# Delta layer: the filter table loaded in four parts, five places to build the filter matrices in, and the key rows of half 0 turned after the filters

## The reference

```
x: [8, 512, 256]; 4 heads of 64; chunks of 32 tokens, 16 to a sequence
q, k, v = silu(conv4(norm(x) @ Wq)), ...              # q, k also scaled to length 1 per head
A  = strictly_lower(-(beta*k) @ k.T); T = inv(1 - A)  # one 32x32 system per sequence, chunk, head
u  = T @ v; w = T @ (beta*k); then a scan over the 16 chunks with the state S
s, m, l = depthwise causal filters of 3, 15, 63 taps over v
out = norm(gate-weighted sum of s, m, l, v and the scan's result) @ Wo
```

## Time and profile before

| | us |
|---|---|
| median of 3 runs | 4577.64 |
| profiled execution | 4567.55 |
| its span | 4565.8 |
| PE busy in the span | 3829.3 (84%) |
| DVE busy | 2545.7 (56%) |
| POOL busy | 2020.5 (44%) |
| ACT busy | 1897.9 (42%) |
| end of the last filter of half 0, of half 1 | 290.0, 509.6 |

### The profile page before, as it was taken

The page is one execution under the profiler, slowest core; times in us unless marked ns, Lnnn a source line. Parts: engine busy times, 40 slices in busy tenths (PEclk is TensorE's granted clock), DMA queues, the critical chain, the costliest instruction groups (busy, mean ns, idle before and its releaser), DMA issues. The chain is left out here.

```text
span 4565.8 us, 70606 instructions
## 1 busy us (share of the span) xinstructions
PE 3829.3 (84%) x26088; PEld 2661.1 (58%) x26088; DVE 2545.7 (56%) x4540; ACT 1897.9 (42%) x3440; POOL 2020.5 (44%) x2061
## 2 busy tenths in 40 slices
PE   5677796799999519958999799788888888999995
PEld 2555774466767319943544455466666666656663
DVE  5566563455454582247777432498888887412223
ACT  3224132333333202225666412488888886112222
POOL 3531463323232216632332211298999998332223
PEclk8788897899999859978999999899999999999997
DMA  4774642200000529954544210111111111822224
GB/s 113 234 226 137 199 120 74 84 5 19 10 19 6 173 70 295 297 152 135 151 138 137 65 63 28 51 50 41 49 47 52 52 47 52 278 92 45 46 46 131
DMA packets 333687, 459.66 MB, mean 101 GB/s; under 512 B 70838, under 2 KB 245366, under 8 KB 329222
## 3 DMA queue, kind: packets, MB, share of 16 engines
q1 hardware_dynamic: 310710, 424.27, 30.5%
q0 software_dynamic: 22512, 30.36, 3.6%
q10 hardware_dynamic: 128, 0.52, 0.0%
HBM read 314.54 MB, written 140.51 MB: 100 GB/s over the span
## 5 line engine op out<-in xcount | busy, mean ns | idle before, releaser
L3565 POOL TENSOR_TENSOR mamba_hC<-mamba_h_t,mamba_cb 128x512 f32<-128x512 f32 x512 | 678.3, 1353 | 68.5 <-DVE mamba_h_t L3078 63.2
L3078 DVE TENSOR_TENSOR_SCAN mamba_h_t<-mamba_dA,mamba_pB 128x512 f32<-128x512 f32 x512 | 597.2, 1207 | 122.8 <-PE mamba_pB L3456 47.1
L3456 PE MATMUL mamba_pB<-ident,mamba_dBT 128*128 128x128 f32 x2048 | 328.8, 285 | 55.0 <-DVE mamba_h_t L3078 49.6
L3254 ACT ACTIVATE mamba_dA<-mamba_delta,mamba_a_neg 128x512 f32<-128x512 f32 x512 | 356.7, 713 | 21.5 <-DVE mamba_h_t L3078 20.9
L3456 PEld LDWEIGHTS mamba_pB<-ident,mamba_dBT 128*128 128x128 f32 x2048 | 240.4, 144 | 190.7 <-issue 99.0
L3465 PE MATMUL mamba_pY<-ident,mamba_hC 128*128 128x128 f32 x2048 | 321.3, 281 | 15.1 <-POOL mamba_hC L3565 14.1
L1911 POOL TENSOR_SCALAR mqa_prob<-mqa_prob,mqa_rinv 128x128 f32<-128x128 f32 (+3 forms) x256 | 136.7, 534 | 424.9 <-DVE mqa_rinv L1687 423.9
L2350 DVE TENSOR_REDUCE mha_nmax<-mha_pM 128x1 f32<-128x384 f32 (+3 forms) x352 | 215.9, 635 | 106.4 <-PE mha_pM L2658 103.2
L3245 ACT ACTIVATE mamba_dBT<-mamba_eT,mamba_b_t 128x512 f32<-128x512 f32 x384 | 273.8, 713 | 0.1
L1501 POOL DMA_INDIRECT top_sum<-top_y,top_xg x71 | 110.4, 1555 | 352.3 <-ACT top_y L1290 341.9
L3465 PEld LDWEIGHTS mamba_pY<-ident,mamba_hC 128*128 128x128 f32 x2048 | 248.1, 145 | 24.2 <-POOL mamba_hC L3565 23.5
(11 more groups left out here) (617 smaller groups left out, 8931.8 us busy)
## 6 DMA issues: line engine op xcount, KB each, us to landing
expert_w<-in_L_ffn_W SPq DMA_DIRECT2D x48, 1024.0 KB, 5.9
delta_shared<-delta_w SPq DMA_DIRECT2D x64, 576.0 KB, 4.9
mamba_cb<-mamba_c SPq DMA_DIRECT2D x128, 256.0 KB, 3.1
mha_qkT<-mha_parts_d SPq DMA_DIRECT2D x96, 256.0 KB, 5.1
delta_w<-delta_wst SPq DMA_DIRECT2D x32, 576.0 KB, 2.8
expert_w<-in_L_ffn_W SPq DMA_DIRECT2D x48, 256.0 KB, 6.4
top_w<-in_L_ffn_w SPq DMA_DIRECT2D x24, 512.0 KB, 10.7
top_slots<-top_y SPq DMA_DIRECT2D x1, 9159.0 KB, 36.5
```

Source lines behind the costliest of these rows:

```text
L3078: nc.vector.tensor_tensor_scan(h_t[:, n % RH, :], dA[:, n % RA, :], pB[n % 2][:, :], 0.0, ALU.mult, ALU.add).then_inc(z["scan_ready"], 1)
L3254: nc.scalar.activation(dA[:, n % RA, :], delta[:, a % 2, ct, :], ACT.Exp, scale=a_neg[:, ct, s:s + 1])\
L3456: last = nc.tensor.transpose(pB[n % 2][:, tok(t)], dBT[:, r % RS, t, ct * P:(ct + 1) * P], c.ident[:, :])
L3565: nc.gpsimd.tensor_tensor(hC[:, n % RO, :], h_t[:, n % RH, :], cb[:, r % RC, :], ALU.mult)\
```

## The change

- The table comes in four parts of 8 groups (`load_table`), 16 DMAs each. Part 0 stands where the whole table stood; then come x of sequence 2, part 1, stores 0 to 3, part 2, stores 4 to 7, x of sequence 3, part 3, stores 8 to 27. Stores 28 to 31 stand behind the beta stores, ahead of `bs`.
- Matrices 0 to 24 are built in five places, two in `wst` and three in `vn`; 25 to 31 in the two of `wst`. GpSimd builds 0 to 2 after variance 1, 3 to 7 after variance 2, the rest after variance 3. `vn` is loaded only when the places in it are stored.
- In both halves v is turned right after the first gram; v is stored ahead of `gs`, and `vn` is loaded right behind the `gs` stores, ahead of `lt`.
- `gs` lies in `sq2`, no longer in `kr`. The memset of the pads of `vp`, which overlaps it, waits for the `gs` stores.
- In half 0 the key rows are turned after the last filter, and copied after the last product and L4603. In half 1 they stay where they were.

The diff, with less indentation and little context:

```diff
@@ -4122,11 +4122,15 @@
   .rearrange("p (f s i) -> p f s i", f=HF, i=CH)
+spare = vn[:, :, :].rearrange("p a d -> p (a d)")[:, 0:3 * WCOLS].rearrange("p (n x) -> p n x", x=WCOLS)
+built_in = [wst[:, 0, :], wst[:, 1, :], spare[:, 0, :], spare[:, 1, :], spare[:, 2, :]]
+place = [g % 5 if g < 25 else (g - 25) % 2 for g in range(FG)]
+turn_of = [place[:g].count(place[g]) for g in range(FG)]
 early = wst[:, :, :].rearrange("p a x -> p (a x)").rearrange("p (n x) -> p n x", x=3 * D)
...
 firT = vr[0:64, :, :].rearrange("p a d -> p (a d)")[:, 0:KD * 3 * P].rearrange("p (k f c) -> p k f c", k=KD, f=3)
-gs = kr[:, NCH // 2:, :].rearrange("p n d -> p (n d)").rearrange("p (a t h i) -> p a t h i", a=NCH // 4, t=4, h=H)
+gs = sq2[:, :, :, :].rearrange("p s k i -> p (s k i)").rearrange("p (a t h i) -> p a t h i", a=NCH // 4, t=4, h=H)
 flat_t = lambda t, q: t[:, q, :, :].rearrange("p j i -> p (j i)")
@@ -4150,8 +4154,8 @@
 ring = lambda name, n: [sc.sem(f"{name}{i}") for i in range(n)]
-x_in, w_st, o_in, xr_in, y_st = (
-  ring(s, 2) for s in ("x_in", "w_st", "o_in", "xr_in", "y_st"))
+x_in, o_in, xr_in, y_st = (ring(s, 2) for s in ("x_in", "o_in", "xr_in", "y_st"))
+w_st, table_in = ring("w_st", 5), ring("table_in", 4)
 te_in = [ring(f"te_in{hf}_", 2) for hf in range(HF)]
@@ -4252,7 +4256,14 @@
           sp.wait_ge(z["w_built"], g + 1)
-          sp.dma_start(w_d[g], wst[:, g % 2, :]).then_inc(w_st[g % 2], 16)
+          sp.dma_start(w_d[g], built_in[place[g]]).then_inc(w_st[place[g]], 16)
+
+        def load_table(part):
+          some = slice(part * FG // 4, (part + 1) * FG // 4)
+          for r in range(R):
+            sp.dma_start(table[C8 * r:C8 * (r + 1), some, :],
+                   h_d.rearrange("(g c) x -> c g x", c=C8)[:, some, R - 1 - r:R - 1 - r + RUN])\
+              .then_inc(table_in[part], 16)
@@ -4318,13 +4329,24 @@
     sp.wait_ge(z["h_st"], 16)
-    for r in range(R):
-      sp.dma_start(table[C8 * r:C8 * (r + 1), :, :],
-             h_d.rearrange("(g c) x -> c g x", c=C8)[:, :, R - 1 - r:R - 1 - r + RUN])\
-        .then_inc(z["table_in"], 16)
+    load_table(0)
+  if a == 2:
+    load_table(1)
+    for g in range(4):
+      store_table(g)
+    load_table(2)
+    for g in range(4, 8):
+      store_table(g)
+  if a == 3:
+    load_table(3)
 if hf == 0:
-  for g in range(3 * FG // 4):
+  for g in range(8, FG - 4):
     store_table(g)
+sp.wait_ge(z["vr_ready"], NCH // 2 * (hf + 1))
+for bb in range(HB):
+  for i in range(CH // R):
+    sp.dma_start(rows_of_runs(v_d, hf, bb, i, 0, NCH), vr[half_lanes(bb, i), :, :])\
+      .then_inc(z["v_st"], 16)
 for i in range(NCH // 4):
@@ -4332,11 +4354,13 @@
       .then_inc(z["g_st"], 16)
-sp.wait_ge(z["vr_ready"], NCH // 2 * (hf + 1))
-for bb in range(HB):
-  for i in range(CH // R):
-    sp.dma_start(rows_of_runs(v_d, hf, bb, i, 0, NCH), vr[half_lanes(bb, i), :, :])\
-      .then_inc(z["v_st"], 16)
+sp.wait_ge(z["v_st"], 16 * HB * CH // R * (hf + 1))
+if hf:
+  sp.wait_ge(z["o_st"], 16 * hf)
+else:
+  for i in range(2, 5):
+    sp.wait_ge(w_st[i], 16 * place.count(i))
+sp.dma_start(vn[:, :, :], runs_of(v_d, hf)).then_inc(z["vn_in"], 16)
 sp.wait_ge(z["g_st"], 64 * NCH // 4 * (hf + 1))
@@ -4345,10 +4369,9 @@
          by_chunk[BETA:BETA + H, :, lanes(bb)]).then_inc(z["beta_st"], 16)
-sp.wait_ge(z["v_st"], 16 * HB * CH // R * (hf + 1))
-if hf:
-  sp.wait_ge(z["o_st"], 16 * hf)
-sp.dma_start(vn[:, :, :], runs_of(v_d, hf)).then_inc(z["vn_in"], 16)
+if hf == 0:
+  for g in range(FG - 4, FG):
+    store_table(g)
 sp.wait_ge(z["beta_st"], 64 * (hf + 1))
@@ -4357,13 +4380,10 @@
 if hf == 0:
-  sp.wait_ge(w_st[g % 2], 16 * (g // 2 + 1))
+  sp.wait_ge(w_st[place[g]], 16 * (turn_of[g] + 1))
 if n >= 3:
...
 sp.dma_start(wr[:, n % 3, :], w_d[g]).then_inc(w_ld[n % 3], 16)
-if hf == 0 and g < 4:
-  store_table(3 * FG // 4 + 2 * g)
-  store_table(3 * FG // 4 + 2 * g + 1)
 if hf == 0 and g % 8 == 4:
@@ -4390,6 +4410,7 @@
   sp.dma_start(a_d.rearrange("n p x -> p n x")[:, some, 2 * D:], vr[:, some, :]).then_inc(z["v_kept"], 16)
+sp.wait_ge(z["kr_ready"], NCH // 2)
 for part in range(2):
@@ -4516,17 +4537,18 @@
           nc.vector.memset(xt[:, :, :, :], 0.0)
-          last = nc.vector.memset(vp[:, :, :, 0:PAD * HB], 0.0)
-          last.then_inc(z["pads"], 1)
-          for i in range(NCH // 2):
-            n = NCH // 2 * hf + i
-            dve.wait_ge(z["kr_ps"], n + 1)
-            if n == NCH // 2:
-              dve.wait_ge(z["kr_kept"], 32)
-            if i == NCH // 4:
-              dve.wait_ge(z["g_st"], 64 * NCH // 4 * (hf + 1))
-            nc.vector.tensor_copy(kr[:, 2 * i:2 * i + 2, :].rearrange("p n d -> p (n d)"), bank[6 + n % 2][:, :])\
-              .then_inc(z["kr_ready"], 1)
+
+          def key_rows():
+            for i in range(NCH // 2):
+              n = NCH // 2 * hf + i
+              dve.wait_ge(z["kr_ps"], n + 1)
+              if n == NCH // 2:
+                dve.wait_ge(z["kr_kept"], 32)
+              nc.vector.tensor_copy(kr[:, 2 * i:2 * i + 2, :].rearrange("p n d -> p (n d)"), bank[6 + n % 2][:, :])\
+                .then_inc(z["kr_ready"], 1)
+
+          if hf:
+            key_rows()
           for s in range(4):
@@ -4539,6 +4561,8 @@
     .then_inc(z["gl_ready"], 1)
+dve.wait_ge(z["g_st"], 64 * NCH // 4 * (hf + 1))
+nc.vector.memset(vp[:, :, :, 0:PAD * HB], 0.0).then_inc(z["pads"], 1)
 for q in range(SQ):
@@ -4703,6 +4729,7 @@
 act.wait_ge(z["qk_kept"], 64)
+act.wait_ge(z["kr_ps"], NCH // 2)
 act.wait_ge(z["o_part"], FQ)
@@ -4744,9 +4771,7 @@
 logits(base + HB - 1)
-if hf:
-  act.wait_ge(z["kr_kept"], 32)
-for i in range(NCH // 4):
+def gram_copies(i):
   n = NCH // 4 * hf + i
@@ -4754,6 +4779,8 @@
                          ACT.Copy).then_inc(z["g_ready"], 1)
+
+          gram_copies(0)
           for i in range(NCH // 2):
@@ -4761,6 +4788,8 @@
              ACT.Copy).then_inc(z["vr_ready"], 1)
+for i in range(1, NCH // 4):
+  gram_copies(i)
 act.wait_ge(z["logit_ready"], base + HB)
@@ -4933,7 +4962,8 @@
           pe.wait_ge(z["xnT_ready"], base + HB)
-          for i in range(NCH // 4):
+
+          def gram(i):
             n = NCH // 4 * hf + i
@@ -4947,6 +4977,7 @@
+gram(0)
 pe.wait_ge(z["c_ready"], 3 * base + PAIRS)
@@ -4959,16 +4990,22 @@
+          for i in range(1, NCH // 4):
+            gram(i)
           pe.wait_ge(z["logit_ready"], base + HB)
-          for i in range(NCH // 2):
-            n = NCH // 2 * hf + i
-            if i >= 2:
-              pe.wait_ge(z["kr_ready"], n - 1)
-            for t in range(2):
-              for k in range(KD):
-                last = nc.tensor.transpose(bank[6 + n % 2][:, t * D + k * P:t * D + (k + 1) * P],
-                               chunk(k_t, k, 2 * i + t), c.ident[:, :])
-            last.then_inc(z["kr_ps"], 1)
+          def turn_keys():
+            for i in range(NCH // 2):
+              n = NCH // 2 * hf + i
+              if i >= 2:
+                pe.wait_ge(z["kr_ready"], n - 1)
+              for t in range(2):
+                for k in range(KD):
+                  last = nc.tensor.transpose(bank[6 + n % 2][:, t * D + k * P:t * D + (k + 1) * P],
+                                 chunk(k_t, k, 2 * i + t), c.ident[:, :])
+              last.then_inc(z["kr_ps"], 1)
+
+          if hf:
+            turn_keys()
@@ -4987,7 +5024,8 @@
-pe.wait_ge(z["kr_ready"], NCH // 2 * (hf + 1))
+if hf:
+  pe.wait_ge(z["kr_ready"], NCH // 2 * HF)
 pe.wait_ge(z["vr_ready"], NCH // 2 * (hf + 1))
@@ -5026,6 +5064,9 @@
+if hf == 0:
+  pe.wait_ge(z["vp_ready"], FQ)
+  turn_keys()
 pe.wait_ge(z["prod_ready"], 3 * FQ * (hf + 1))
@@ -5149,12 +5190,13 @@
-if g >= 2:
-  pool.wait_ge(w_st[g % 2], 16 * (g // 2))
+pool.wait_ge(table_in[4 * g // FG], 16 * R)
+if turn_of[g]:
+  pool.wait_ge(w_st[place[g]], 16 * turn_of[g])
 for f in "lms":
...
   last = nc.gpsimd.tensor_tensor(
-    wst[:, g % 2, WCOL[f]:WCOL[f] + n * C8].rearrange("p (x c) -> p x c", c=C8),
+    built_in[place[g]][:, WCOL[f]:WCOL[f] + n * C8].rearrange("p (x c) -> p x c", c=C8),
     table[:, g, FIRST[f]:FIRST[f] + n].unsqueeze(2).to_broadcast([P, n, C8]),
@@ -5169,13 +5211,15 @@
   variance(HB * hf + bb)
-  if hf == 0 and bb == HB - 2:
+  if hf == 0 and bb == 1:
     pool.wait_ge(z["ones"], 1)
-    pool.wait_ge(z["table_in"], 16 * R)
-    for g in range(4):
+    for g in range(3):
+      matrix(g)
+  if hf == 0 and bb == 2:
+    for g in range(3, 8):
       matrix(g)
 if hf == 0:
-  for g in range(4, FG):
+  for g in range(8, FG):
     matrix(g)
```

More of the change, by code:

```diff
@@ L4140, in stage_delta @@
         NS, PAIR = HF * NCH, HF * NCH // 2
-        NAMES = ("late_in", "small_in", "fir_in", "wq_in", "wk_in", "wv_in", "cleared", "setup", "bias", "f_ps", "f_sb", "h_ps", "h_sb", "h_st", "table_in", "w_built", "xn_done",
+        NAMES = ("late_in", "small_in", "fir_in", "wq_in", "wk_in", "wv_in", "cleared", "setup", "bias", "f_ps", "f_sb", "h_ps", "h_sb", "h_st", "w_built", "xn_done",
```

## The result

| | before | changed |
|---|---|---|
| median of 4 runs each, us | 4574.42 (4567.22 to 4577.68) | 4530.91 (4519.97 to 4536.55) |
| profiled execution, us (span) | 4567.55 (4565.8) | 4533.55 (4531.5) |
| granted clock, whole span | 0.923 | 0.925 |

The ratio is 0.9904, 95% interval 0.9884 to 0.9924: faster, by 35 to 53 us, about 1%. The forecast was a gain of 24 us and a time of 4554; 4530.9 lies under the low end of its range, 4537.

The account below looks back on a forecast made before the run. Half 0 was taken to be bound by a serial chain of table, GpSimd and queue. Half 0's −26 us, key rows +0.5 and half 1 +1.5 gave −24: 4577.6 to 4554 us, range 4537 to 4570.

Parts of the forecast that it names:

- The chain that the prediction named: Half 0: a serial chain of table, GpSimd and queue, not TensorE, sets when the first filter starts, 185.35 us before.
- x of sequence 3 used: Half 0: this load becomes the late one, used at 76 us (67 to 84), VectorE standing still from 59.
- stores 28, 29 issued; matrices 30, 31 built: Half 0: four late stores ahead of bs add a new wait; issue at 156 us, matrices built by 169.
- filter stage: Half 0's filters, with no stores left among them, take 89 us (84 to 95) and end at 264.
- key rows: Half 0's key copies, moved behind its end, hide in VectorE's wait for half 1's x; cost 0.5 us.
- half 1: New order there: vn 4 us earlier, lt, beta and bs 2 to 3 later; net +1.5 us (−2 to +5).
- The table: Half 0's table load: 0.7 us per quarter DMA, 10.4 us per part at 69 GB/s, part 0 landed about 38.
- the wait behind `vn`: Half 0: stores 28 and 29 land 8.3 us after issue, holding matrices 30 and 31 until 164 us.
- the second rival: Half 0's filter stage stays 104.7 us because its waits are for DRAM traffic; total 4570 us; chance 12%.
- The first: Table load: each DMA costs 2.14 us whatever its size, so the kernel is slower, 4613 us; chance 5%.
- third rival: Half 0: freer queue, late stores landing in 5 us, filters from 161 to 245; total 4535 us; chance 20%.
- spread over more DMA engines: Table load: by the skill's rule eight-partition parts spread no wider; over sixteen, 5 us each, x of sequence 3 16 us earlier.

Follow-up runs that it names:

- run 4: The changed kernel with half 0's key rows turned and copied at their old place, ahead of the gates: 4530.99 us.
- run 1: The kernel before with only its table loaded in 64 quarter DMAs, all partition sets for one quarter, then the next: 4564.15 us against 4578.63.
- run 6: The kernel before with the table in 64 quarter DMAs, each changing both partitions and quarter: 4554.71 us.
- run 5: The kernel before with the table in 64 quarter DMAs, the four quarters of the same eight partitions in a row: 4555.4 us.
- run 10: The changed kernel timed again, unedited, beside the kernel before: 4531.82 us over 6 runs, ratio 0.9908.
- run 3: The changed kernel with all matrices built in two places instead of five: 4554.83 us against 4578.63 for the kernel before.
- run 12: The kernel before profiled a second time, unedited: 4572.55 us.

## Why the prediction was wrong

The chain that the prediction named is the one that moved, and one size in it was off. Step by step:

| step | forecast, us | measured, us |
|---|---|---|
| one table DMA on the queue | 0.7 (0.54 to 2.14) | 0.35 to 0.46 |
| part 0 landed, GpSimd begins | 38 | 33.25 |
| x of sequence 3 used | 76 (67 to 84) | 64.72 |
| v stored from | 129 | 118.44 |
| vn issued | 148 | 139.44 |
| stores 28, 29 issued; matrices 30, 31 built | 156; 169 | 143.07; 157.9 |
| bs landed, first filter | 174, 175 | 161.07, 163.75 |
| filter stage | 89 (84 to 95) | 90.0 |
| last filter of half 0 | 264 | 253.76 |
| key rows | +0.5 | nothing that shows (run 4) |
| half 1 | +1.5 | +1.4, within the spread of 219.1 to 221.1 |

**The failed step is "The table".** It took 0.7 us per DMA and 10.4 us per part "because the table's issues are held by its traffic", and carried the old rate, 69 GB/s, over to the parts. The issues did take longer where the traffic was slower, but its rate is not a property of the table: it came from staying on eight partitions for 174 KB. Four parts are also a new order of writing, and in that order the table moves at 119 to 120 GB/s (runs 1 and 6 against 5). Even the low end, 0.54, was too high: it is a quarter of the old price, and just what run 5 pays (34.79/64), in which the old rate stays. The whole issue fell from 34.24 to 25.7 us, and x of sequence 3, behind three parts and eight stores, came 11.3 us before the forecast. That load is where the wrong rate did most: the prediction let the traffic of three parts and eight stores hold it until 73. In the trace GpSimd ends matrix 7 at 55.32, and the queue issues its store at 55.34 and x at 55.80, so GpSimd alone set it, and GpSimd had begun 4.75 us before the forecast. The first filter came 11.25 us before its forecast. The intermediate steps went with it to within 3 us: the wait behind `vn` was a little longer than the row taken (stores 28 and 29 hold GpSimd until 153.01, 9.9 us after their issue, against 8.3), lt and beta were quicker, and bs landed 2.8 us after issue, not 5.0. These cancel.

**The filter stage** was forecast at 89 us and took 90.0 (92.4 in run 10). In the kernel before, the late stores stand between the loads of the first four groups, and these took 26.6 us; in the change they take 11.5 (163.75 to 175.23), while the other 28 take 78.5 us where they took 78.1. Run 1, which has the stores still in this stage, needs 105.2 us, and 27.4 of them for the first four groups. Run 4, with the key rows back, and run 3, with two places, keep a stage of 92.1 and 91.4. So it is the stores that cost some 15 us, though no run moves them alone, and the second rival (the stage stays at 104.7) is out. Not all of the 15 us was waiting: TensorE was busy for 15.64 us of the first four groups at a granted clock of 0.69, and is for 10.42 at 0.84. The stage now waits for its own loads: in the window of the loop TensorE is busy 75.48 of 90 us at 246 GB/s, not far from the 251 of the earlier trace rows.

```profile
164.00:254.00 90.00, 75.48 (x604) 72.99 (x605) 69.49 (x91) 5.66 (x10) 39.59 (x29) 0.94 0.77 246
```

**The rivals.** The first (2.14 us whatever the size) is out: 0.35. The Trainium skill ("DMA: Bandwidth & Descriptors", "Bandwidth") counts transfers under 64 KB as dominated by their descriptors and advises larger ones; its figures are for loads to 128 partitions issued from GpSimd. These loads, of eight partitions each from SyncE's queue, go the other way: 64 DMAs of 43.5 KB took 24.69 us (run 1) and 16 of 174.0 KB 34.24. The third rival comes nearest: it had x of sequence 3 at 67, v at 120 and the first filter at 161. Its faults are late stores that land in 5 us, where it took 9.9, and a filter stage of 84. The last filter of the trace, 253.76, lies between the forecast's 264 and rival 3's 245.

The prediction asked whether a part would spread over more DMA engines. Nothing in the trace says that it did: the DMA share went down, from 0.59 to 0.49 (run 1), and the gain was in the time of a packet.

**From 34 to 43 us.** In the traces half 0 ends at 290.04 and 295.79 before, at 253.76 and 256.16 changed (runs 10 and 12): 38.0 us between the means. Half 1: 512.7 against 475.9, 36.8 us. The next stage begins its loads at 733.53 and 738.67 before, at 703.07 and 703.27 changed: 32.9 us between the means. But between the last filter of half 1 and these loads there are 221.0 to 229.7 us in the fourteen traces, whatever the version, so this place is told less well than the end of half 1. The medians gained 43.5 and 41.1.

So of the 19.5 us between the gain forecast, 24, and the 43.5 of the medians, 10.8 are in the delta layer of the profiled pair (34.8 at the end of half 1), and that is the table. Another 2.0 come with the second pair of traces: the first profile of before was quick. No trace of the delta layer shows the other 6.7; they lie within the interval of the medians (34.8 to 49.4 in run 10). The code behind the delta layer is the same, and takes 3828.4 and 3839.5 us in two executions of the changed kernel: whether it gained anything stays open.

The table alone did not carry the time out of the range. A gain of 34.8 us would have given 4577.6 − 34.8 = 4542.8, above 4537. That 4530.9 was measured takes the 8.7 us above as well, and 3.2 us by which the median of before fell, from 4577.64 over three runs to 4574.42 over four. So the failed step is a true error of 10.8 us, and that the range was missed is partly chance.

## What to carry to other kernels

When a transfer is cut up, don't carry its rate over from the whole: ask which partitions each piece writes and what stands before and behind it. For a load that goes down in blocks of a few partitions, try it cut along its other dimension, the block changing from one DMA to the next, even if nothing consumes it in parts: here that alone ended half 0 19.5 us sooner. And in a serial chain of queue, VectorE and GpSimd, look for what stands last at each joint: here cutting the table left the wait at the next load and at the late stores, and moving two stores, one load and three matrices was worth another 15 to 19 us beside the 43.5 of the change.

## What the hardware showed that was not expected

- 2.85 MB in 16 DMAs of 174.0 KB to eight partitions each: 34.24 us of issue, 66 GB/s, DMA share 0.59. In 64 DMAs with the partitions changing: 24.69 and 24.93 us, 119 and 120 GB/s, share 0.49 and 0.48. In 64 with the partitions kept for four: 34.79 us, 67 GB/s, 0.60.
- The rate beats with the stay on eight partitions: near 50 GB/s, with peaks of 78 to 107 some 2.6 to 3.2 us apart, in DMAs of 174.0 KB and in four of 43.5 KB alike.
- A busy DMA share was no sign of a rate at its limit: the share fell from 0.59 to 0.49 while the rate rose to 1.8 times. A packet kept an engine busy for 92 ns before and for 41 in run 1.
- The first 16 DMAs of 43.5 KB took 0.35 us each of the queue (5.57/16), the last 16 of the change 0.46 (7.37/16), and with the partitions kept 0.54 (34.79/64).
- Half 0 of the same kernel ended 5.75 us apart in two executions, and the rest of the program behind the delta layer 11 us apart, so a single pair of profiles tells a gain of 40 us to some 10. The first filter of half 0, ahead of all this, repeated within 0.5 us (185.35 and 184.88 before, 163.75 and 163.76 changed).
